# Layer norm of a recurrence writes its rows into the tile of the bounded rows, and the next load waits for the norm instead of the store

## The chip, the cores and the metric

One core of one Trainium2 chip runs the whole program: a TensorE (PE), a VectorE (DVE), a ScalarE (ACT), a GpSimd (POOL) and a SyncE (SP), which in this kernel only issues DMAs. The metric is the device time of one execution in microseconds (us).

## What is computed

Four layers on 2048 tokens of 512 channels, all in float32, each followed by a residual addition and a layer norm:

```python
x = layernorm(x + mamba2(x))              # first stage
x = layernorm(x + bounded_product(x))     # second stage, first half
x = layernorm(x + rg_lru(x))              # second stage, second half
x = layernorm(x + gated_ffn(x))           # third stage
```

The second stage, where the change lies, computes this:

```python
out = (x @ weight) * scale
n = max(norm(out), eps);  out = out * tanh(n) / (n + eps)
out = out * min(0.99 / max(norm(out), eps), 1)      # the bounded rows
x = layernorm(x + out)

y = gelu(x @ w_y + b_y);  xb = x @ w_x + b_x        # rg_lru
conv = causal convolution of xb over 4 tokens
gate_x, gate_a = sigmoid(conv @ w_ig + b_ig), sigmoid(conv @ w_ag + b_ag)
a = exp(-8 * gate_a * softplus(a_param));  mult = sqrt(1 - a**2)
h[t] = a[t] * h[t-1] + gate_x[t] * conv[t] * mult[t]
x = layernorm(x + (h * y) @ w_out + b_out)
```

## The kernel before, in words

The program has three stages, written as generators of instructions for each engine: `mamba2`, `bounded_rg_lru` and `gated_ffn`. The tokens go from stage to stage through HBM (tensors `tokens0`, `tokens1`). The order of the work on each engine is written out by hand, and engines are kept in step by counting semaphores. Every product is made of three passes over high and low parts of its operands (names that end in h and l).

The stage of the change is `bounded_rg_lru`. It works on NS = 8 pieces of 256 tokens, each of C = 2 chunks (j = 0, 1) of 128 tokens; pieces alternate between the two sequences. The loops of the engines' `main` run over steps s = 0 to 7, and a step mixes work for several pieces. The rows of a piece live in a row buffer, `slot(s)`, one of SLOTS = 3 tiles `c_xb` of 128 partitions x 2 chunks x 512. What happens to a piece p there:

- SP loads it from `tokens0` into its slot (`load_x`, L1091). Pieces 0 to 2 are loaded ahead; piece p = q + 3 takes the slot of piece q.
- In step p - 2 PE transposes its rows (`turn_in`, L1449), as the last work of the step; ACT copies the high part (L1201), DVE makes the low part (L1296).
- In step p - 1 PE multiplies it with the bounded layer's weights (L1456); DVE scales the result into the tile `ob` (`scaled`, L1301); ACT squares `ob` (L1206); POOL makes the bounding factors (L1135 to L1146); DVE adds the bounded row from `ob` to the row in the slot (`bounded`, L1308) and finishes that layer norm in place (`bounded_out`, L1317). From here `ob` is not used until the next step. PE transposes the slot again (`turn`, L1474), ACT and DVE make the parts `xth`, `xtl` (L1215, L1322), and POOL adds the output bias to the slot (L1161).
- In step p PE makes the four projections in the order x, y, ag, ig (`project`, L1486), with the bounded product of the next piece after x and the output product of the previous piece (`output`, L1456) after y. The ag projection waits for the convolution's high part `cvh` (ACT, L1263), the turn of the next piece stands between ag and ig.
- ACT makes the gates (L1224), the decay (L1233) and the square root (L1279). In step p + 1 DVE runs the recurrence (`recur`, L1350 to L1357), and late in the same step adds the product to the row in the slot (`norm`, L1368), and its last operation finishes the layer norm in place (`norm_out`, L1378).
- SP stores the finished rows from the slot to `tokens1` (`store`, L1096).

DVE's order in a step s is: recurrence of s - 1, `scaled` of s + 1, convolution of s (L1329), `bounded` and `bounded_out` of s + 1, `norm` and `norm_out` of s - 1, `turn` of s + 1, `turn_in` of s + 2, the square for the decay (L1344); at the end of steps 5 and 6 four conversions of the third stage's weight codes follow (`convert`, L1767).

ACT's order around the end of a step is: sigmoid of the ig projection (two halves, written to `gx`), the decay, the high part of `turn_in`, the square root.

SP has one queue of its own: `main` in its `sync` issues store(s) and then load_x(s + 3) for s = 0 to 4, store(5), then the next stage's transfers with store(6) and store(7) between them. The load of each chunk waits until the store of the same chunk has landed:

```python
wait(sp, s_st[j], 16 * (s - SLOTS + 1))
sp.dma_start(slot(s)[:, j, :], chunk(x_in, s, j)).then_inc(s_x[s % SLOTS][j], 16)
```

`wait` is a helper that emits nothing when the value is not positive. `order` makes the next instruction of an engine wait for the previous one. The third stage waits, before its first results are written, until all stores of the second have landed; its tile `d_sg` lies in the place of `ob`, and its residual tiles in the places of slots 0 and 1.

Of the kernel before, what the change touches and what calls it, by code (L numbers as in the profile page):

```python
# [12 lines left out]
ALU = mybir.AluOpType  # L13
# [36 lines left out]
class Again:  # L50
# [5 lines left out]
    def wait(self, eng, count):  # L56
        eng.wait_ge(self.sem, self.value + count)
# [939 lines left out]
def bounded_rg_lru(nc, signals, psum, ident, powers, x_in, x_out, scale, vectors, b_out, W, split, last, spaces, room, ahead):  # L997
# [7 lines left out]
    C = T // P  # L1005
    NT = x_in.shape[0] // (B * C)
    NS = B * NT
    M = KD
    SLOTS = 3
    TINY = 1e-7  # L1010
    LIMIT = 0.99
    def sem(name):
        return signals("c_" + name)
# [3 lines left out]
    for i in range(2):  # L1017
# [6 lines left out]
    ob = sb("c_ob", [P, C, D], F32)  # L1024
# [11 lines left out]
    mv = sb("c_mv", [P, C, 4], F32)  # L1036
# [29 lines left out]
    s_st = [sem(f"st{j}") for j in range(C)]  # L1066
# [7 lines left out]
    s_hy, s_hyh, s_hyl, s_bo, s_out, s_res, s_var, s_std, s_ln = (  # L1074
        sem(n) for n in ("hy", "hyh", "hyl", "bo", "out", "res", "var", "std", "ln"))
    s_dve, s_pool = sem("dve_order"), sem("pool_order")

    def chunk(dram, s, j):
        return dram[s % B * NT * C + s // B * C + j]
# [4 lines left out]
    def slot(s):  # L1084
        return xb[s % SLOTS]

    def sync(sp):
        def load_x(s):
            for j in range(C):
                wait(sp, s_st[j], 16 * (s - SLOTS + 1))  # L1090
                sp.dma_start(slot(s)[:, j, :], chunk(x_in, s, j)).then_inc(s_x[s % SLOTS][j], 16)  # L1091

        def store(s):
            for j in range(C):
                sp.wait_ge(s_ln, C * s + j + 1)
                sp.dma_start(chunk(x_out, s, j), slot(s)[:, j, :]).then_inc(s_st[j], 16)  # L1096

        def constants():
            sp.dma_start(vec, vectors).then_inc(s_small, 16)
            sp.dma_start(scl, scale.partition_broadcast(P)).then_inc(s_small, 16)  # L1100

        def main(following_stage):
            sp.wait_ge(*last["output"])
            sp.dma_start(bo, b_out.partition_broadcast(P)).then_inc(s_bias, 16)
            load_x(2)
            for dst, src, arrived in ahead:
                sp.dma_start(dst, src).then_inc(arrived, 16)
            for s in range(NS - 2):
                store(s)
                if s + SLOTS < NS:  # L1110
                    load_x(s + SLOTS)
            following_stage["small"]()
            following_stage["load_x"](0)
            following_stage["gate_codes"]()
            store(NS - 2)
            following_stage["up_codes"]()
            following_stage["load_r"](0, 0)
            following_stage["load_r"](0, 1)
            store(NS - 1)
            following_stage["down_codes"]()  # L1120
            for j in range(C):
                sp.wait_ge(s_st[j], 16 * NS)

        return {"load_x": load_x, "constants": constants, "main": main}

    def gpsimd(pool):
# [163 lines left out]
    def vector(dve):  # L1290
# [7 lines left out]
        def scaled(s):  # L1298
            for j in range(C):
                dve.wait_ge(s_bm, C * s + j + 1)  # L1300
                dve.tensor_tensor(ob[:, j, :], ps_o[:, j, :], scl, ALU.mult).then_inc(s_ob, 1)  # L1301

        def bounded(s):
# [70 lines left out]
        def norm_out(s):  # L1374
            for j in range(C):
                out = slot(s)[:, j, :]
                dve.wait_ge(s_std, C * s + j + 1)
                dve.tensor_scalar(out, out, mv[:, j, 0:1], mv[:, j, 2:3], ALU.subtract, ALU.mult).then_inc(s_ln, 1)  # L1378

        z = vec[:, AP, :]  # L1380
        e, u, l, one, q, k8 = (spt[:, i, :] for i in range(6))
# [19 lines left out]
        def main(following_stage):  # L1401
            dve.wait_ge(s_const, 1)
            for s in range(NS):
                if s:
                    recur(s - 1)
                    low_hy(s - 1)
                if s + 1 < NS:
                    scaled(s + 1)
                convolve(s)
                low_conv(s)  # L1410
                if s + 1 < NS:
                    bounded(s + 1)
                    bounded_out(s + 1)
                else:
                    following_stage["front"](0, (0, 1))
                if s:
                    norm(s - 1)
                    norm_out(s - 1)
                if s + 1 < NS:
                    turn(s + 1)  # L1420
                if s + 2 < NS:
                    turn_in(s + 2)
                if s + 1 == NS:
                    following_stage["front"](0, (2, 3))
                squared(s)
                if NS - 4 < s < NS - 1:
                    for i in range(4 * (s - NS + 3), 4 * (s - NS + 4)):
                        following_stage["convert"](i)
# [3 lines left out]
            for m in range(1, EARLY):  # L1432
                following_stage["product"](0, m)
            norm(NS - 1)
            norm_out(NS - 1)

        return {"turn_in": turn_in, "softplus": softplus, "scaled": scaled, "bounded": bounded, "bounded_out": bounded_out,
                "turn": turn, "main": main}

    def tensor(pe):  # L1440
# [58 lines left out]
        def main(following_stage):  # L1499
# [37 lines left out]
            "bias": (s_bo, C * NS), "gate_a": s_ga, "gate_x": s_gx, "n_gate": M * (NS - 1), "residual": s_res, "n_residual": C * (NS - 1),  # L1537
            "stored": s_st, "n_stored": 16, "steps": NS, "order": (s_dve, s_pool)}
    return (sync, gpsimd, scalar, vector, tensor), uses


# [336 lines left out]
def build(nc, x, out, d):  # L1878
# [7 lines left out]
    with ExitStack() as ctx:  # L1886
# [7 lines left out]
        for n, name in (("b", "weight"), ("x", "w_in1"), ("y", "w_y"), ("ag", "w_ag"), ("ig", "w_ig"), ("out", "w_out1")):  # L1894
# [9 lines left out]
        assert ends[0] == scan_at and place.at <= scan_at and late.at <= ends[1]  # L1904
        room["scan"] = scan_at
        second, last_second = bounded_rg_lru(nc, signals, psum, ident, powers, between[0], between[1], d["scale"], d["vectors"], d["b_out"], W,
                                dict(zip(W, parts)), last, ((place.at, scan_at), (ends[1], codes[0])), room,
                                [(dst, src, s_codes) for dst, src in transfers])
# [96 lines left out]
```

## Time and profile before

| what | value |
|---|---|
| three runs | 1181.51, 1182.25, 1185.72 us |
| median | 1182.25 us |
| the profiled execution, its own time | 1180.73 us |
| its span in the profile | 1178.9 us |
| PE busy | 1088.4 us (92%) |
| PE weight loads busy | 946.0 us (80%) |
| DVE busy | 748.2 us (63%) |
| ACT busy | 574.1 us (49%) |
| POOL busy | 320.2 us (27%) |
| share of the 16 DMA engines taken by SP's queue | 20.2% |

The span is the time from the first to the last recorded instruction; the execution's own time is 1.8 us longer. The first stage ends its PE work around 465 us, the stage of the change runs from there to about 805 us, the third stage to the end. Matmul durations overlap, since PE is pipelined; the starts of successive instructions tell more than their lengths.

### The profile page before, as it was taken

How to read it: one execution, taken by the hardware profiler on the slowest of the kernel's cores; microseconds unless marked ns; L12 is line 12 of the kernel's file. 1: busy time of each engine (PE TensorE's matmuls, PEld its weight loads, DVE VectorE, ACT ScalarE, POOL GpSimd, SP SyncE). 2: the span in 40 equal slices, each digit the busy share in tenths (PEclk: the TensorE clock that was granted, in tenths of full speed). 3: DMA queues.
4: the chain of work that ended last, by engine and by line, in shares of the span. 5: the costliest groups of instructions: out<-in, count | busy, mean ns of one | idle time of the engine just before them, and what ended most of it. 6: DMA issues, size and time to landing. Idle time of an engine off the chain costs nothing.

```text
span 1178.9 us, 18136 instructions
## 1 busy us (share of the span) xinstructions
PE 1088.4 (92%) x6912; PEld 946.0 (80%) x6912; DVE 748.2 (63%) x1307; ACT 574.1 (49%) x1190; POOL 320.2 (27%) x437
## 2 busy tenths in 40 slices
PE   6889999999999997599999999899999999999997
PEld 6778787978888885489898898887878878878876
DVE  6899999899999997548666776765332233223213
ACT  6866656666666654355666466563302311321320
POOL 1021213030312214453435344413302311321331
PEclk9899999999999998799999999989999999999999
DMA  5513131231303046220111101408012002002001
GB/s 189 194 41 101 46 96 51 91 104 38 122 20 122 7 147 229 94 95 1 37 37 37 36 1 36 136 18 285 1 36 72 1 18 90 1 1 72 1 1 54
DMA packets 41590, 81.22 MB, mean 69 GB/s; under 512 B 7456, under 2 KB 13472, under 8 KB 39456
## 3 DMA queue, kind: packets, MB, share of 16 engines
q1 hardware_dynamic: 41504, 80.06, 20.2%
q8 instruction: 55, 0.90, 0.3%
q14 instruction: 31, 0.25, 0.1%
HBM read 67.19 MB, written 12.85 MB: 68 GB/s over the span
## 4 chain that ended last, share of the span: by engine, by line
PE 64%; DVE 15%; ACT 10%; issue 5%; DMA 3%; POOL 3%; SPq 0%; DVEq 0%; POOLq 0%; ACTq 0%
PE banks L1836 20%; PE banks L799 17%; PE banks L1847 10%; PE banks L1486 7%; PE banks L1456 4%; DVE a_xs L698 2%; PE banks L879 1%; ACT a_xs L451 1%; DVE c_gx L1353 1%; PE banks L929 1%; DMA c_wxraw<-in_w_in 1%; DVE a_xs L691 1%; DVE a_L L675 1%; ACT c_a L1233 1%; DMA c_xb<-tokens 1%
## 5 line engine op out<-in xcount | busy, mean ns | idle before, releaser
L1737 ACT ACTIVATE d_sg<-banks,d_gs 128x512 f32<-128x512 f32 x64 | 44.0, 688 | 249.2 <-PE banks L1836 249.2
L1779 DVE SCALAR_TENSOR_TENSOR d_h<-banks,d_us,d_sg 128x512 f32<-128x512 f32 x64 | 48.0, 751 | 161.5 <-PE banks L1836 149.1
L1711 POOL TENSOR_TENSOR d_hl<-d_h,d_hh 128x512 fp32r<-128x512 f32 x64 | 83.1, 1298 | 156.0 <-ACT d_hh L1741 156.0
L1847 PE MATMUL banks<-d_wd,d_hh 128*128 128x512 f32 x256 | 104.1, 407 | 2.9 <-POOL d_hl L1711 2.9
L578 DVE SCALAR_TENSOR_TENSOR a_xs<-a_xpre,a_cvec,a_xs 128x256 f32<-128x256 f32 x192 | 100.3, 538 | 6.3 <-ACT a_xs L451 1.8
L1847 PE MATMUL banks<-d_wd,d_hl 128*128 128x512 f32 x256 | 103.6, 405 | 0.0
L327 POOL TENSOR_TENSOR a_sg<-a_sg 128x512 f32<-128x512 f32 x16 | 21.6, 1347 | 231.2 <-ACT a_sg L443 231.2
L661 DVE TENSOR_TENSOR_SCAN a_L<-a_L,a_ident 128x512 f32<-128x512 f32 x64 | 78.4, 1224 | 2.2
L467 ACT ACTIVATE a_xdt<-banks,a_dt 128x64 f32<-128x64 f32 x256 | 56.3, 349 | 47.2 <-PE banks L879 47.2
L799 PE MATMUL banks<-a_xth,a_wxh 128*128 128x256 f32 x256 | 75.9, 297 | 0.0
L799 PE MATMUL banks<-a_xth,a_wgh 128*128 128x256 f32 x256 | 74.7, 292 | 0.0
L799 PE MATMUL banks<-a_xtl,a_wxh 128*128 128x256 f32 x256 | 73.3, 286 | 0.0
L799 PE MATMUL banks<-a_xth,a_wxl 128*128 128x256 f32 x256 | 73.2, 286 | 0.0
L799 PE MATMUL banks<-a_xth,a_wgl 128*128 128x256 f32 x256 | 72.6, 283 | 0.0
L799 PE MATMUL banks<-a_xtl,a_wgh 128*128 128x256 f32 x256 | 72.5, 283 | 0.0
L1847 PEld LDWEIGHTS banks<-d_wd,d_hh 128*128 128x128 f32 x256 | 50.0, 196 | 14.8 <-POOL d_hl L1711 3.3
L799 PE MATMUL banks<-a_woh,a_ygh 128*128 128x512 f32 x128 | 57.5, 449 | 2.8 <-DVE a_ygl L704 2.8
L1847 PEld LDWEIGHTS banks<-d_wd,d_hl 128*128 128x128 f32 x256 | 49.8, 195 | 11.7
L1785 DVE TENSOR_TENSOR d_tmp<-banks,d_dsb 128x512 f32<-128x512 f32 x16 | 11.1, 691 | 75.5 <-PE banks L1847 75.5
L799 PE MATMUL banks<-a_woh,a_ygl 128*128 128x512 f32 x128 | 55.4, 432 | 0.0
L799 PE MATMUL banks<-a_wol,a_ygh 128*128 128x512 f32 x128 | 55.0, 430 | 0.0
L799 PEld LDWEIGHTS banks<-a_xth,a_wxh 128*128 128x128 f32 x256 | 49.7, 194 | 4.7 <-issue 4.0
(284 smaller groups left out, 3196.3 us busy)
## 6 DMA issues: line engine op xcount, KB each, us to landing
a_L<-decays SPq DMA_DIRECT2D x16, 1024.0 KB, 5.2
a_xf<-in_x SPq DMA_DIRECT2D x16, 256.0 KB, 2.9
a_xr<-in_x SPq DMA_DIRECT2D x16, 256.0 KB, 2.7
tokens<-a_xr SPq DMA_DIRECT2D x16, 256.0 KB, 4.2
c_xb<-tokens SPq DMA_DIRECT2D x16, 256.0 KB, 2.8
tokens<-c_xb SPq DMA_DIRECT2D x16, 256.0 KB, 2.0
d_xin<-tokens SPq DMA_DIRECT2D x16, 256.0 KB, 4.7
d_r<-tokens SPq DMA_DIRECT2D x16, 256.0 KB, 2.7
```

Source lines behind the costliest of these rows:

```text
L467: ins = act.activation(xdt[:, j, h * HD:(h + 1) * HD], ps_t[:, q % 2, 2 * j + i // 2, i % 2 * HD:(i % 2 + 1) * HD], ACT.Copy, scale=dt[:, ...
L578: ins = dve.scalar_tensor_tensor(out=dst, in0=src[:, k:k + T], scalar=vec[:, k:k + 1], in1=dst, op0=ALU.mult, op1=ALU.add)
L661: order(dve.tensor_tensor_scan(own, own, ident4.rearrange("p h t -> p (h t)"), 0.0, ALU.mult, ALU.add))
L698: dve.tensor_tensor(own, own, sg[:, :, cols(j)], ALU.mult).then_inc(s_yg, 1)
L799: last = pe.matmul(out, lhs(i, k), rhs(c, k), start=(k, i, c) == (0, 0, 0), stop=(k, i) == (n - 1, 1))
L1456: done = pe.matmul(ps_x, x[:, k, cols(j)], wp[:, k, :], start=i == 0, stop=i == 3 * KD - 1)
L1486: done = pe.matmul(ps_x[:, q, m % 2, :], wp[:, k, m * P:(m + 1) * P], x[:, k, :], start=i == 0, stop=i == 3 * KD - 1)
L1711: pool.tensor_tensor(hl[:, m, :], h32[:, m % 2, :], hh[:, m, :].bitcast(F32), ALU.subtract).then_inc(s_hl, 1)
L1737: act.activation(sg[:, m % 2, :], ps_g[:, m % 2, :], ACT.Silu, scale=gs[:, m:m + 1]).then_inc(s_sg, 1)
L1779: dve.scalar_tensor_tensor(out=h32[:, m % 2, :], in0=ps_u[:, m % 2, :], scalar=us[:, m:m + 1], in1=sg[:, m % 2, :], op0=ALU.mult, op1=ALU. ...
L1836: ins = pe.matmul(out[:, m % 2, :], w(k, m), x[:, k, :], start=(k == 0 and x is xth), stop=(k == KD - 1 and x is xtl))
L1847: ins = pe.matmul(ps_o[:, c % 2, :], h[:, m, cols(c)], wd[:, m, :], start=(m == 0 and h is hh), stop=(m == M - 1 and h is hl))
```

## The change

The last operation of the layer norm (`norm_out`) writes pieces 0 to 4 into `ob` instead of the slot, and SP stores those from `ob`. Pieces 5 to 7 are written and stored as before. The load into the slot waits for `norm_out` of the old piece and no longer for its store, and SP issues it ahead of that store. `scaled`, which is the next to write `ob`, gets a wait for that store.

```diff
     def slot(s):
         return xb[s % SLOTS]
 
+    def finished(s):
+        return ob if s + SLOTS < NS else slot(s)
+
     def sync(sp):
         def load_x(s):
             for j in range(C):
-                wait(sp, s_st[j], 16 * (s - SLOTS + 1))
+                wait(sp, s_ln, C * (s - SLOTS) + j + 1)
                 sp.dma_start(slot(s)[:, j, :], chunk(x_in, s, j)).then_inc(s_x[s % SLOTS][j], 16)
 
         def store(s):
             for j in range(C):
                 sp.wait_ge(s_ln, C * s + j + 1)
-                sp.dma_start(chunk(x_out, s, j), slot(s)[:, j, :]).then_inc(s_st[j], 16)
+                sp.dma_start(chunk(x_out, s, j), finished(s)[:, j, :]).then_inc(s_st[j], 16)
...
             for s in range(NS - 2):
-                store(s)
                 if s + SLOTS < NS:
                     load_x(s + SLOTS)
+                store(s)
...
         def scaled(s):
             for j in range(C):
                 dve.wait_ge(s_bm, C * s + j + 1)
+                wait(dve, s_st[j], 16 * (s - SLOTS + 1))
                 dve.tensor_tensor(ob[:, j, :], ps_o[:, j, :], scl, ALU.mult).then_inc(s_ob, 1)
...
-                dve.tensor_scalar(out, out, mv[:, j, 0:1], mv[:, j, 2:3], ALU.subtract, ALU.mult).then_inc(s_ln, 1)
+                dve.tensor_scalar(finished(s)[:, j, :], out, mv[:, j, 0:1], mv[:, j, 2:3], ALU.subtract, ALU.mult).then_inc(s_ln, 1)
```

## Rows read from the trace of the kernel before

**Rows 1.** The page: the span, and the chain that ended last by engine.

```profile
span 1178.9 us, 18136 instructions
PE 64%; DVE 15%; ACT 10%; issue 5%; DMA 3%; POOL 3%; SPq 0%; DVEq 0%; POOLq 0%; ACTq 0%
```

**Rows 2.** The chain of waits in order of time (start us, us, what), 530 to 800 us.

```profile
561.29 2.02 DMA tokens<-c_xb
563.33 2.71 DMA c_xb<-tokens
566.08 0.66 PE banks L1449 x4
...
635.52 2.00 DMA tokens<-c_xb
637.54 2.88 DMA c_xb<-tokens
640.46 0.66 PE banks L1449 x4
...
710.07 2.00 DMA tokens<-c_xb
712.09 2.64 DMA c_xb<-tokens
714.77 0.65 PE banks L1449 x4
```

**Rows 3.** Waits of PE, the whole span (us in total, times, longest us).

```profile
PE banks L1449 <- DMA c_xb<-tokens: 7.1, 9, 1.6
```

**Rows 4.** Timeline of PE, second chunk of turn_in at the end of steps 2 and 4.

```profile
602.56 0.65 PE L1449 MATMUL banks<-ident,c_xb 128*128 128x128 f32 x4 [0.75 <-DMA c_xb<-tokens]
...
677.50 0.66 PE L1449 MATMUL banks<-ident,c_xb 128*128 128x128 f32 x4 [0.79 <-DMA c_xb<-tokens]
```

**Rows 5.** Timeline of ACT, the last ig gate of steps 0 to 6.

```profile
527.07 0.84 ACT L1224 ACTIVATE c_gx<-banks,c_vec 128x256 f32<-128x256 f32 x2 [2.00 <-PE banks L1486]
...
563.12 0.84 ACT L1224 ACTIVATE c_gx<-banks,c_vec 128x256 f32<-128x256 f32 x2 [2.00 <-PE banks L1486]
...
601.33 0.84 ACT L1224 ACTIVATE c_gx<-banks,c_vec 128x256 f32<-128x256 f32 x2 [2.00 <-PE banks L1486]
...
638.02 0.84 ACT L1224 ACTIVATE c_gx<-banks,c_vec 128x256 f32<-128x256 f32 x2 [2.00 <-PE banks L1486]
...
675.90 0.84 ACT L1224 ACTIVATE c_gx<-banks,c_vec 128x256 f32<-128x256 f32 x2 [2.00 <-PE banks L1486]
...
712.96 0.84 ACT L1224 ACTIVATE c_gx<-banks,c_vec 128x256 f32<-128x256 f32 x2 [2.00 <-PE banks L1486]
...
750.23 0.84 ACT L1224 ACTIVATE c_gx<-banks,c_vec 128x256 f32<-128x256 f32 x2 [2.00 <-PE banks L1486]
```

**Rows 6.** Timeline of DVE: norm_out of the second chunk, steps 1 and 3.

```profile
560.72 0.55 DVE L1378 TENSOR_SCALAR c_xb<-c_xb,c_mv 128x512 f32<-128x512 f32 x1 [0.71 <-POOL c_mv L81]
...
634.95 0.55 DVE L1378 TENSOR_SCALAR c_xb<-c_xb,c_mv 128x512 f32<-128x512 f32 x1 [0.71 <-POOL c_mv L81]
```

**Rows 7.** Timeline of the weight loads: PE's wait for cvh in step 1.

```profile
550.21 0.53 PEld L1486 LDWEIGHTS banks<-c_cvh,c_wagh 128*128 128x128 f32 x4 [0.29 <-ACT c_cvh L1263]
```

**Rows 8.** Timeline, steps 5 and 6: conversion, bounded_out (DVE), turn (PE).

```profile
719.75 0.68 DVE L1767 TENSOR_SCALAR d_wg_early<-d_wg_early_codes 128x1024 fp32r<-128x1024 int32 x1
...
742.97 0.55 DVE L1317 TENSOR_SCALAR c_xb<-c_xb,c_bmv 128x512 f32<-128x512 f32 x1 [0.72 <-POOL c_bmv L81]
...
743.48 1.03 PE L1474 MATMUL banks<-ident,c_xb 128*128 128x128 f32 x8
```

**Rows 9.** Timeline: scaled in step 5, PE's wait for hyl in step 7.

```profile
691.58 1.28 DVE L1301 TENSOR_TENSOR c_ob<-banks,c_scl 128x512 f32<-128x512 f32 x2
...
767.11 0.80 PE L1456 MATMUL banks<-c_wouth,c_hyh 128*128 128x512 f32 x1 [4.68 <-DVE c_hyl L1361]
```

**Rows 10.** DMA issues of two lines with their times to landing.

```profile
L1091 SPq DMA_DIRECT2D c_xb<-tokens x16: 319/320/1757, 436.7 to 712.1; - x16
...
DMA to landing us min/median/max: 2.6/2.8/10.7
...
L1659 SPq DMA_DIRECT2D d_xin<-tokens x16: 430/432/2561, 750.5 to 990.1; - x16
...
DMA to landing us min/median/max: 2.7/4.7/11.9
```

**Rows 11.** Stretches, steps 1 and 2: length, busy PE PEld DVE ACT POOL, PEclk, DMA, GB/s.

```profile
527.00:563.00 36.00, 35.96 (x257) 33.35 (x255) 25.64 (x48) 21.84 (x40) 14.69 (x24) 1.00 0.04 16
563.00:601.00 38.00, 35.66 (x256) 33.29 (x256) 25.61 (x48) 22.06 (x40) 15.45 (x24) 1.00 0.11 37
```

## The prediction
> **What bounds the kernel now.** The page's chain that ended last comes first: PE holds 64% of it, and DMA 3% [rows 1]. The chain in order of time then says where those DMAs are. In the stage of the change it has three passes of one form, at 561, 636 and 710 us: a store of 2.0 us, at once the load that waited for it (2.6 to 2.9 us), and then PE's `turn_in` [rows 2]. The list of PE's waits gives the price: `turn_in` waited 7.1 us for these loads in total [rows 3]. That is a ceiling seen from PE; seen from the chain the ceiling is its three stores, 2.02 + 2.00 + 2.00 = 6.0 us, since a chain can't become shorter than what is cut from it. No other wait inside the steps 1 to 6 is of that size; after them PE waits 4.7 us for the recurrence [rows 9], which hangs on the gates of step 6. So what decides is how much earlier step 6 ends.
>
> I measure the stage by G(n), the start of the last ig gate on ACT in step n, which follows the last ig matmul at once: G(0) to G(6) are 527.07, 563.12, 601.33, 638.02, 675.90, 712.96, 750.23 [rows 5]. Four quantities make them:
>
> - Step 0 to 1 had its load early, and its length of 36.05 is a **floor** for every step. Its first ag weight load still waited 0.29 us for `cvh` [rows 7], so PE alone would be near 35.7.
> - The loop over ACT, DVE and POOL: `norm_out` of the second chunk ends 561.27 and 635.50 [rows 6], that is G(n-1) + 34.2 both times (561.27 - 527.07, 635.50 - 601.33).
> - From that end to T, the start of `turn_in`'s second chunk: 566.08 - 561.27 = 4.81, 640.46 - 635.50 = 4.96 [rows 2, 6].
> - From T to the next G: 35.25, 35.46, 35.44, 35.46, 35.46 (601.33 - 566.08 to 750.23 - 714.77) [rows 2, 4, 5].
>
> So a step's G depends on the G two steps earlier: 34.2 + 4.9 + 35.4 = 74.5 us for two steps, where the floor is 72.1. PE and the DVE loop nearly balance, and the store sits on the link between them.
>
> **The change part by part.** *The load no longer waits for the store*: five pairs of loads (pieces 3 to 7). The interval from `norm_out` to T loses its store, so it is 2.8 to 3.0 us. I go through the steps, T' and G' being the new times:
>
> - Step 1: T' = 561.27 + 2.79 = 564.06, G'(2) = 564.06 + 35.25 = 599.3.
> - Step 2: T' = 563.12 + 34.2 + 2.96 = 600.3, G'(3) = 635.7.
> - Step 3: T' = 599.3 + 34.2 + 2.96 = 636.5, G'(4) = 671.9.
> - Step 4: T' = 635.7 + 34.2 + 3.03 = 672.9, G'(5) = 708.4.
> - Step 5: T' = 671.9 + 34.2 + 2.72 = 708.8, and by the same rule G'(6) = 744.3.
>
> The floor holds in all of them within 0.2 us (599.3 - 563.1 = 36.2 and so on). **What is late next** is in step 6. Four conversions of about 0.6 us stand before its recurrence on DVE [rows 8], so `bounded_out`'s second chunk ended at 743.52, G(5) + 30.56, just as PE's `turn` began with the first chunk at 743.48. G'(5) comes 4.5 us earlier, but PE reaches `turn` 5.9 us earlier and must wait for that row. From the second half of `turn` (0.4 after 743.48) to 750.23 are 6.3 us, so G'(6) = 708.4 + 30.56 + 6.3 = 745.3. That is 750.23 - 745.3 = 4.9 us of gain, and 5.9 without this wait.
>
> After G(6) everything in the stage follows from the gates, PE even has its 4.7 us of slack before `hyl` [rows 9], and the third stage runs on PE back to back, so the shift goes through whole. PE's granted clock is already 1.00 in these steps [rows 11], so nothing is won or lost there: what PE did before is the same.
>
> *The store moves behind the load in SP's order.* SP issues two loads, then two stores, 0.32 us each. The load of the second chunk was alone in flight, or nearly; now two stores leave 0.3 and 0.6 us behind it. Nearest rows: the load of the first chunk today goes out while the second chunk's store is in flight, and all loads of this line have a median of 2.8; four loads issued in a row (`d_xin`) land after 2.7 at least and 4.7 in the median [rows 10]. So between 0 and +1.9 us for each load, and I take 0.05, because what is behind it in the queue should hardly hurt the transfer ahead, and the 2.7 is the nearest row. Three of them are on the chain: 0.15. The stores themselves land up to 1 us later, read by nobody in time.
>
> The Trainium skill, "DMA: Bandwidth & Descriptors", section on latency and other measured facts, puts an HBM access at 0.2 us on average and 2 us at high load. If the two stores made such a load, the landing would grow by up to 1.8 us and an estimate by it would leave almost no gain; the first-chunk loads of today's trace, which meet a store and don't show it, speak against that.
>
> *`scaled` gets a wait*: for pieces 3 to 7, two chunks, ten waits on DVE. Behind it on DVE stand the convolution and all that follows. The store leaves at G(n-1) + 34.2 + about 0.7 and lands 2 us later, near G(n) + 1; `scaled` runs at G(n) + 15.7 (691.58 - 675.90) [rows 9]. The wait is met with some 14 us to spare. A satisfied wait has no row of its own; it costs between 0 and the 0.1 us of the smallest gaps in the chain, I take 0.03, for six of them on the path 0.2 us.
>
> *`norm_out` writes another tile*: same shape and type, 0.55 us [rows 6], nothing. `ob` is free there: its readers, ACT's square and DVE's `bounded`, come earlier in the same step.
>
> **Sum.** 4.9 - 0.15 - 0.2 = 4.55 us. The profiled execution took 1180.73, so 1176.2; the median of the runs stands 1.5 us above it, which gives 1182.25 - 4.6 = 1177.6.
>
> **The rivals.**
>
> - *A, the whole chain*: PE's new wait in step 6 doesn't appear, or the loads land a little faster, and the gain is the three stores, 6.0: 1176.2. For it: 7.1 us of PE's waits are there to be removed. Against it: `bounded_out` in step 6 is fixed by DVE.
> - *B, the loads pay back part*: the stores right behind them cost each load on the chain 0.8 us, 2.4 in all, leaving 2.3: 1180.0. The median of 4.7 for four in a row speaks for it, the pair's 2.8 against.
> - *C, slower*: the same place, worse. From 4.7 / 3 = 1.6 us more per load on, the gain is gone; if a load with two stores beside it takes double, 5.6 instead of 2.8, the sum is 3 x 2.8 - 4.7 = 3.7 us slower: 1186.0. The largest landing of this line, 10.7 us, was with megabytes of weights in flight [rows 10], where now there are two stores.
> - *D, no effect*: the load was not what held PE, for instance because PE waits as long for `cvh` and `turn` instead: 1182.3. The waits of 0.29 us in the only step without a late load [rows 7] speak against more than a tenth of it.
>
> **How the numbers follow.** 0.5% is 5.9 us, about what a measurement of this kernel can tell from no change. The forecast has 0.55 (own range, 4.0 to 5.4 of gain: 1176.8 to 1178.3), A 0.20, B 0.13, C 0.05, D 0.07. The gain's ceiling of 6.0 lies at that bound, so "faster" is half of A and, with the 1.5 us between execution and median, a part of the forecast: 0.25. "Slower" is most of C: 0.04. The rest, 0.71, is "same", though I expect a real gain there. The range reaches from a little under A, 1175.2, to past B, 1180.8; out of it stay C and D and a tail of A, 0.2 in all.
>
> **What the profile would show.** Right: SP's load is issued within 0.1 us of `norm_out`'s end; the chain has no DMA `tokens<-c_xb` in this stage; PE's wait at L1449 falls from 7.1 to about 2 us; G spacings near 36.2; PE waits 0.5 to 1.5 us at L1474 in step 6; G(6) near 745.5; landings of L1091 stay 2.6 to 2.9. Wrong: landings over 3.5 us (B, C); new waits of PE at L1474 or L1486 in every step (D); DVE waiting for a DMA at L1301; or G(6) moved by 4.6 and the end not, which would mean that the third stage waits for something of its own.

## The result, and the profile after

| | before | changed |
|---|---|---|
| runs | 1181.51, 1182.25, 1185.72, 1185.07 us | 1175.85, 1175.38, 1176.04, 1174.91 us |
| median | 1183.66 us | 1175.62 us |
| the profiled execution, its own time | 1180.73 us | 1175.85 us |
| its span | 1178.9 us | 1174.1 us |
| PE busy | 1088.4 us | 1085.9 us |

The ratio is 0.9932, with a 95% interval from 0.991 to 0.9954. The changed kernel is faster by 8.0 us between the medians, but by 4.8 us of span between the two profiled executions. These are two findings. The traces can explain the second number directly; what lies between it and the first is taken up below.

The chain of waits of the changed kernel in order of time (start us, us, what), 590 to 810 us, answers to [rows 2]:

```profile
597.05 3.30 DMA c_xb<-tokens
600.35 0.04 issue
600.39 0.65 PE banks L1453 x4
...
670.04 2.97 DMA c_xb<-tokens
673.01 0.04 issue
673.05 0.66 PE banks L1453 x4
...
724.47 0.90 issue
725.36 1.28 DVE c_ob L1305 x2
726.64 1.59 DVE c_cv L1333 x4
...
731.67 1.07 ACT c_cvh L1266
732.76 1.24 DVE c_cvl L1341
734.00 0.04 issue
734.04 5.06 PE banks L1490 x40
```

No store is in it any more, and two loads are left where there were three pairs of store and load. But a load now takes 3.30 and 2.97 us where it took 2.64 to 2.88. The last lines show the new last wait, in step 6: PE stands at the ag projection until DVE's convolution and its low part are there. (Line numbers are 3 to 4 higher than before: L1453 is `turn_in`, L1490 `project`, L1382 `norm_out`.)

PE's waits of the changed kernel, 526 to 750 us (us in total, times, longest us), say the same:

```profile
PE banks L1453 <- DMA c_xb<-tokens: 3.4, 5, 1.1
PEld banks L1490 <- ACT c_cvh L1266: 0.7, 2, 0.5
PEld banks L1490 <- DVE c_cvl L1341: 0.7, 3, 0.3
```

Against [rows 3], 7.1 us fell to 3.4, and the small waits of the weight loads (PEld) for `cvh` and `cvl`, 0.3 and 0.2 us before, grew to 0.7 each.

The timeline of ACT, the last ig gate of steps 0 to 6, answers to [rows 5]:

```profile
526.74 0.84 ACT L1227 ACTIVATE c_gx<-banks,c_vec 128x256 f32<-128x256 f32 x2 [2.00 <-PE banks L1490]
...
562.82 0.84 ACT L1227 ACTIVATE c_gx<-banks,c_vec 128x256 f32<-128x256 f32 x2 [2.00 <-PE banks L1490]
...
599.79 0.84 ACT L1227 ACTIVATE c_gx<-banks,c_vec 128x256 f32<-128x256 f32 x2 [2.00 <-PE banks L1490]
...
635.85 0.84 ACT L1227 ACTIVATE c_gx<-banks,c_vec 128x256 f32<-128x256 f32 x2 [2.00 <-PE banks L1490]
...
672.34 0.84 ACT L1227 ACTIVATE c_gx<-banks,c_vec 128x256 f32<-128x256 f32 x2 [2.00 <-PE banks L1490]
...
708.50 0.84 ACT L1227 ACTIVATE c_gx<-banks,c_vec 128x256 f32<-128x256 f32 x2 [2.00 <-PE banks L1490]
...
745.68 0.84 ACT L1227 ACTIVATE c_gx<-banks,c_vec 128x256 f32<-128x256 f32 x2 [2.00 <-PE banks L1490]
```

From G(0) to G(6) are 218.94 us; before they were 223.16. So 4.2 of the 4.8 us arise here. Another 0.3 us lie ahead of G(0) (527.07 and 526.74) and 0.3 us after G(6) (428.67 and 428.42), where the change does nothing. Other executions differ there by more: a second trace of the changed kernel has 426.71 us after G(6) and a span of 1172.7 (experiment 1), a second one of the kernel before 427.05 and 1179.4 (experiment 11). So the 4.2 us of the stage are the firm number, and the 4.8 us are one pair of executions; the four spans taken crosswise differ by 4.8 to 6.7 us. In the sections below, "the stage" is this distance from G(0) to G(6).

DVE's timeline of the changed kernel at the end of step 2, and then SP's, show the new order:

```profile
596.48 0.55 DVE L1382 TENSOR_SCALAR c_ob<-c_xb,c_mv 128x512 f32<-128x512 f32 x1 [0.71 <-POOL c_mv L81]
```

```profile
595.79 1.58 SPq L1094 DMA_DIRECT2D c_xb<-tokens  x2
597.42 0.90 SPq L1099 DMA_DIRECT2D tokens<-c_ob  x2
```

The first load goes out right after the first chunk's layer norm, the second at 597.05, 0.02 us after the second one's end (596.48 + 0.55), and the two stores 0.4 us behind it.

### The profile page after: what moved, and what is told of

Same layout as the page of the kernel before. It is cut to its first block, busy times and chain, and to the rows that moved or that the text cites. A ratio compares the mean times of both kernels' runs of the same rounds, so it can differ in the third digit from the quotient of the medians.

```text
span 1174.1 us, 18146 instructions
## 1 busy us (share of the span) xinstructions
PE 1085.9 (92%) x6912; PEld 943.6 (80%) x6912; DVE 747.9 (64%) x1307; ACT 574.3 (49%) x1190; POOL 323.4 (28%) x437
## 4 chain that ended last, share of the span: by engine, by line
PE 62%; DVE 17%; ACT 10%; issue 5%; DMA 2%; POOL 2%; SPq 0%; DVEq 0%; POOLq 0%; ACTq 0%
PE banks L1840 20%; PE banks L799 17%; PE banks L1851 11%; PE banks L1490 7%; PE banks L1460 2%; DVE a_xs L698 2%; DVE c_cv L1333 2%; PE banks L879 1%; ACT a_xs L451 1%; DVE c_gx L1357 1%; PE banks L929 1%; ACT c_a L1236 1%; DMA c_wxraw<-in_w_in 1%; DVE a_xs L691 1%; DVE a_L L675 1%
```

## The experiments

The experiments ran in four sets (1 to 4, 5 to 8, 9 to 11, and 12), each on a chip of its own together with runs of the kernel before, which had medians of 1182.33, 1182.43, 1183.08 and 1183.17. Each median is compared with the one of its own set. "The stage" is read from each one's trace.

**1. The changed kernel again.** No edit.

> The changed kernel once more, paired with the kernel before in five rounds. The two traces differ by 4.8 us of span (1178.9 and 1174.1), of which 4.2 us arise between the gates of step 0 and step 6; the medians differ by 8.0. Theory 1, the link alone: the difference of the medians comes out near 4.8 (ratio 0.996). Rival: the kernel before has something besides that the two profiled executions don't show, such as loads that land late in some executions, and the difference stays near 8 (ratio 0.993), with its runs scattered over 3 to 4 us and those of the changed kernel within 1.5 us.

The median was 1175.51 (six runs, 1174.29 to 1176.06), that of the kernel before 1182.33 (22 runs, 1180.46 to 1189.3), the ratio 0.9933 (0.9911 to 0.9954). So the difference of 7 us is real, and of these two kernels the one before is the one that scatters: its shortest runs are 5 us above the changed kernel's median, its longest 14. The stage took 219.04 us, as in the first trace of the changed kernel.

**2. Only the tile and the new wait.**

```diff
-                wait(sp, s_ln, C * (s - SLOTS) + j + 1)
+                wait(sp, s_st[j], 16 * (s - SLOTS + 1))
...
             for s in range(NS - 2):
+                store(s)
                 if s + SLOTS < NS:
                     load_x(s + SLOTS)
-                store(s)
```

> Only the tile of norm_out and the new wait of scaled are kept; the load again waits for the store and stands behind it. Theory 1: nothing is gained, the time is that of the kernel before within 1.5 us, the load goes out 2.0 us after the store of its chunk, and PE waits about 7 us at turn_in. DVE waits for no store at scaled. Rival, the changed destination or the free slot is itself worth or costs something: more than 2 us from the kernel before.

Ratio 0.9999 (0.9982 to 1.0016), stage 223.28 us, PE's wait at `turn_in` 7.5 us. Writing to `ob` and ten more waits on DVE cost nothing that can be measured and bring nothing. So the gain comes from when the load goes out.

**3. The stores first.**

```diff
             for s in range(NS - 2):
+                store(s)
                 if s + SLOTS < NS:
                     load_x(s + SLOTS)
-                store(s)
```

> The whole change but for SP's order: both stores are issued, then both loads, which wait for the layer norm alone. The load of the second chunk, the one on the chain, goes out 1.0 to 1.3 us after norm_out instead of at once (two issues of 0.32 to 0.43 us more), with both stores ahead of it in the queue. Theory 1: its way from norm_out to turn_in takes 4.0 to 4.5 us, 0.8 to 1.2 more than in the changed kernel, and three such ways make it 2.5 to 3.5 us slower than the changed kernel. Rival, the order is nothing and only the wait counted: within 1 us of the changed kernel.

Median 1177.95 (nine runs, 1175.8 to 1182.17), 2.4 us over the changed kernel of the same set; stage 221.15 against 219.04 us. SP's timeline of this kernel at the end of step 1, and then PE's:

```profile
560.20 1.58 SPq L1099 DMA_DIRECT2D tokens<-c_ob  x2
561.82 0.94 SPq L1094 DMA_DIRECT2D c_xb<-tokens  x2
```

```profile
564.88 1.39 PE L1453 MATMUL banks<-ident,c_xb 128*128 128x128 f32 x8 [1.65 <-DMA c_xb<-tokens]
```

The second load goes out near 562.3, 0.9 us after `norm_out`'s end (560.88 + 0.55 = 561.43), and the loads on the chain land after 3.27, 3.08 and 2.98 us. A start 0.8 us later on a way that the chain takes three times makes 2.4 us. The order on SP is worth a third of the change by the medians (2.4 of 6.8 us) and half of it by the stage (2.1 of 4.2).

**4. No loads at all.** Pieces 3 to 7 are not loaded; they are computed from what the slot holds.

```diff
             for s in range(NS - 2):
-                if s + SLOTS < NS:
-                    load_x(s + SLOTS)
                 store(s)
...
         def turn_in(s):
             for j in range(C):
-                pe.wait_ge(s_x[s % SLOTS][j], 16 * (s // SLOTS + 1))
+                if s < SLOTS:
+                    pe.wait_ge(s_x[s][j], 16)
+                else:
+                    pe.wait_ge(s_ln, C * (s - SLOTS) + j + 1)
```

(In `bounded`, DVE's own wait for these loads is left out too.)

> The loads of pieces 3 to 7 are left out, and PE's turn_in and DVE wait for the layer norm of the old piece instead; those pieces are computed from what the slot holds. It gives the end of this road: the link without any DMA. Theory 1: every step takes the floor of 36.05 us, or 35.9 to 36.3, so steps 1 to 6 take 3 us less at most than in the changed kernel (whose gates of steps 1 to 6 are 182.9 us apart), 180.3 to 181.5, and the time is 1.3 to 2.6 us under the changed kernel's. PE waits for cvh and cvl by 0.3 to 0.8 us in each step and not for turn_in. Rival, DMA is still the bound of the stage: 4 us or more are gained.

Median 1173.04 (four runs, 1171.93 to 1176.43), stage 217.57 us, gates of steps 1 to 6 181.49 us apart. PE's waits in it:

```profile
PEld banks L1492 <- ACT c_cvh L1264: 2.5, 6, 0.5
PEld banks L1492 <- DVE c_cvl L1340: 1.5, 6, 0.3
```

All spacings but the last are 36.03 to 36.09 us, the last, with the conversions in front of it, is 37.26. So the floor of 36.05 is real; the only wait that PE has in each of its steps is the one for the convolution's two parts, and the changed kernel is 1.4 us of stage from this one. With nothing left to load, the store's removal could not have brought more than 223.16 - 217.57 = 5.6 us of stage.

**5. Stores held until the loads have landed.**

```diff
                 if s + SLOTS < NS:
                     load_x(s + SLOTS)
+                    sp.wait_ge(s_x[s % SLOTS][1], 16 * ((s + SLOTS) // SLOTS + 1))
                 store(s)
```

> The changed kernel, but SP issues the two stores only when both loads have landed, so that the loads are alone in flight. It measures what the stores right behind the loads cost. In the changed kernel the way from norm_out's end to turn_in's second chunk was 3.36, 3.36 and 3.04 us where steps 1, 2 and 4 waited, against 2.7 to 2.9 from issue to landing of a load that was alone. Theory 1: the way falls back to 2.8 to 3.0 us, the gates of steps 1 to 6 come 0.5 to 1.2 us closer (floor of 36.05 in every step), and the time falls by as much. Rival, the load is slower for another reason (it reads at once what was just written, or its issue): the way stays at 3.3.

The loads of the chain land after 2.77 and 2.76 us again, from 3.30 and 2.97; PE's wait at `turn_in` is 2.1 us from 3.4; the stage 218.22 from 218.94. The median was 1173.63 (four runs, 1172.04 to 1176.92), ratio 0.9928 (0.9905 to 0.9951), which overlaps the changed kernel's interval: a gain of the whole time is not shown. The loads bear the step out in other traces: the seven on the chain with stores right behind them (the changed kernel twice, experiment 6) took 2.97 to 3.33 us, the four with held stores (this one and experiment 8) 2.69 to 2.77. So the stores right behind the load cost it 0.2 to 0.6 us. The ten stores from `ob` took 3.6 us in the median in the changed kernel and 2.3 here.

**6. The conversions moved, in the changed kernel.**

```diff
                 if s + 1 < NS:
                     turn(s + 1)
+                if NS - 4 < s < NS - 1:
+                    for i in range(4 * (s - NS + 3), 4 * (s - NS + 4)):
+                        following_stage["convert"](i)
                 if s + 2 < NS:
                     turn_in(s + 2)
                 if s + 1 == NS:
                     following_stage["front"](0, (2, 3))
                 squared(s)
-                if NS - 4 < s < NS - 1:
-                    for i in range(4 * (s - NS + 3), 4 * (s - NS + 4)):
-                        following_stage["convert"](i)
```

> The changed kernel with the eight conversions of the third stage's codes moved on DVE ahead of the low part of turn_in, where DVE sits idle 5 us in each step for ACT, instead of after the square for the decay. Theory 1: with the store out of the link the DVE loop is what spaces the steps, and four conversions of 0.6 us stood in it in step 5 and four, 3.6 us, in step 6. Step 5 to 6 (37.2 us between gates in the changed kernel) falls to about 36.1, the recurrence of step 6 comes about 2 us earlier after the last gate, and the time falls by 2.5 to 3.5 us. Rival, PE is the bound there anyway and the conversions are hidden: within 1 us of the changed kernel.

The trace shows the places as foreseen: step 5 to 6 took 36.65 us instead of 37.18, and the recurrence of step 6 began 7.4 us after G(6) instead of 9.1. From G(0) to PE's output product in step 7 the trace has 233.46 us instead of 235.81. Yet the median, 1174.63 (1172.27 to 1176.17), is only 0.9 us under the changed kernel's; with a ratio of 0.9929 (0.9913 to 0.9945) the two can't be told apart. The expectation of 2.5 to 3.5 us was missed in the runs; up to that product the trace shows 2.4.

**7. The same move in the kernel before.**

> The same move of the conversions in the kernel before the change. Theory 1: in step 6 the same 2 us, in step 5 less or nothing of the rest, because there the load is what the step waited for only until its turn_in and the conversions come after it: 1.5 to 3.5 us under the kernel before. If it gains the same as in the changed kernel, the two are additive; if nothing, the store's link covered the conversions.

Median 1178.91 against 1182.43, ratio 0.997 (0.9959 to 0.9982): 3.5 us faster. Why the same move brings 3.5 us here, and nothing clear of noise in experiment 6, is not shown. Its trace brought the surprise of this study. The stage took 226.93 us, with spacings of 40.45 and 39.64 us for steps 1 to 2 and 3 to 4, where the code is that of the kernel before, which had 38.21 and 37.88. PE's timeline of `turn_in` at the end of step 1 and after it:

```profile
563.64 0.66 PE L1449 MATMUL banks<-ident,c_xb 128*128 128x128 f32 x4 [1.84 <-DMA c_xb<-tokens]
565.29 0.66 PE L1449 MATMUL banks<-ident,c_xb 128*128 128x128 f32 x4 [0.99 <-DMA c_xb<-tokens]
565.70 0.88 PE L1486 MATMUL banks<-c_xth,c_wxh 128*128 128x256 f32 x4
566.37 1.06 PE L1486 MATMUL banks<-c_xth,c_wxl 128*128 128x256 f32 x4
567.23 1.05 PE L1486 MATMUL banks<-c_xtl,c_wxh 128*128 128x256 f32 x4
568.08 1.05 PE L1486 MATMUL banks<-c_xth,c_wxh 128*128 128x256 f32 x4
568.94 0.89 PE L1486 MATMUL banks<-c_xth,c_wxl 128*128 128x256 f32 x4
569.67 0.64 PE L1486 MATMUL banks<-c_xtl,c_wxh 128*128 128x256 f32 x4
```

Groups of four matmuls start 0.86 us apart from 566.4 to 569 and 0.47 us apart from 569.7 on. The granted clock of 566.1 to 569.5 us is 0.50: TensorE ran at its lower level, 1.2 GHz, for some 3 us after it had stood idle twice for the loads (1.84 and 0.99 us), and then at 2.4 GHz again; from `turn_in` to the next gate are 37.0 us (602.29 - 565.29) instead of 35.25, so this fall cost 1.7 us.

**8. Both, the moved conversions and the held stores.**

> Both, the moved conversions and the held stores, on top of the change. Theory 1: the gains add up where the floor leaves room, 3 to 4.5 us under the changed kernel, and the gates of steps 1 to 6 are 180.3 to 181 us apart. Rival: one of the two replaces the other, 2.5 us or less.

Median 1171.47 (five runs, 1170.97 to 1172.87), ratio to the kernel before 0.9908 (0.9892 to 0.9923), 2.2 under experiment 5 of the same set and 4.0 us under the changed kernel's 1175.51, which is of another set (none of its runs is as short as this version's longest). The stage took 217.34 us, and its gates of steps 1 to 6 are 181.29 apart. This version is the fastest of the study and computes the same.

**9. PE kept busy in the wait, in the kernel before.**

```diff
-                pe.wait_ge(s_x[s % SLOTS][j], 16 * (s // SLOTS + 1))
...
+                if s >= SLOTS:
+                    for k in range(6 - 2 * j):
+                        pe.transpose(ps_t[:, j, k % KD, :], ident, ident)
+                pe.wait_ge(s_x[s % SLOTS][j], 16 * (s // SLOTS + 1))
```

(the wait for the load is moved behind the wait for the bank and the spare transposes.)

> The kernel before, but PE runs ten spare transposes of the identity (six ahead of the first chunk, four ahead of the second) where it stands idle for the loads of pieces 3 to 7. Clock theory: in some executions of the kernel before, TensorE's granted clock falls to half for 3 us after the wait at turn_in (seen in the trace of the run with the conversions moved in the kernel before: 0.96 over steps 1 to 2 and 3 to 4, matmuls of 128x256 at 0.21 us instead of 0.12 from 566 to 570 us), which makes such a step 1.7 us longer; that is why its runs spread over 5 to 9 us, and why the medians lie 7 apart and the traces 4.8. With the idle time filled, the clock stays at 1.00, the runs spread over 3 us or less, and the median comes down 1.5 to 2.5 us, to 1180 to 1181, without the load coming earlier. Rival, the spread comes from DMA: the same median and spread as the kernel before.

The median was 1183.3, the ratio 1.0001 (0.9984 to 1.0018), the runs 1179.15 to 1186.45. The trace has a granted clock of 1.00 in every step and, once, a store of the chain that took 3.75 us instead of 2.0. So what the clock theory expected did not come: PE's waits at `turn_in` fell to 4.0 us, from 7.1 to 7.7, and the median did not come down. Its stage took 225.22 us in this trace, 2.1 more than in the first trace of the kernel before, 1.75 of them by that one store; whether the spare transposes lengthen other executions is not known, so the theory is weakened and not refuted.

**10. One longer wait, in the kernel before.**

```diff
                 wait(sp, s_st[j], 16 * (s - SLOTS + 1))
+                wait(sp, s_st[C - 1], 16 * (s - SLOTS + 1))
```

> The kernel before, but the load of the first chunk waits for both stores, so it goes out 1.3 us later and PE's wait at turn_in is in one piece, 0.5 to 3 us, instead of two. Clock theory: the granted clock falls in two or three of the steps in each execution, and the median rises by 3 us or more, of which the later load itself explains 1 at most (0.3 us a step on the second chunk). Rival without a clock: 1 us slower or less.

Median 1185.02, ratio 1.0017 (1.0002 to 1.0032), 1.9 us slower. In the trace PE's timeline at the end of step 1 reads:

```profile
565.51 0.66 PE L1450 MATMUL banks<-ident,c_xb 128*128 128x128 f32 x4 [3.08 <-DMA c_xb<-tokens]
566.59 0.65 PE L1450 MATMUL banks<-ident,c_xb 128*128 128x128 f32 x4 [0.42 <-DMA c_xb<-tokens]
567.00 1.10 PE L1487 MATMUL banks<-c_xth,c_wxh 128*128 128x256 f32 x4
567.89 1.05 PE L1487 MATMUL banks<-c_xth,c_wxl 128*128 128x256 f32 x4
568.75 1.05 PE L1487 MATMUL banks<-c_xtl,c_wxh 128*128 128x256 f32 x4
569.60 1.05 PE L1487 MATMUL banks<-c_xth,c_wxh 128*128 128x256 f32 x4
570.46 0.68 PE L1487 MATMUL banks<-c_xth,c_wxl 128*128 128x256 f32 x4
```

After 3.08 and 0.42 us of idle time the clock fell to 1.2 GHz, and the step took 41.09 us. It fell in one step of this execution, not in two or three, and the 1.9 us lie between what the clock theory expected (3 or more) and the rival (1 or less).

**11. The kernel before once more.**

> The kernel before once more with a profile, for a second look at it. Clock theory: if its time is over 1183, its trace shows a step of 38.5 us or more between gates with a granted clock under 1.00; if it is near 1180.5, none does. The loads land after 2.8 us in the median either way. Rival: a slow execution has late loads or a longer first or third stage.

Its profiled execution took 1181.18 us. Steps 1 to 5 are like those of [rows 5], but step 5 to 6 took 39.61 us instead of 37.27. PE's timeline there:

```profile
713.94 0.66 PE L1449 MATMUL banks<-ident,c_xb 128*128 128x128 f32 x4 [1.24 <-DMA c_xb<-tokens]
715.33 1.08 PE L1449 MATMUL banks<-ident,c_xb 128*128 128x128 f32 x4 [0.73 <-DMA c_xb<-tokens]
716.05 1.20 PE L1486 MATMUL banks<-c_xth,c_wxh 128*128 128x256 f32 x4
717.06 1.05 PE L1486 MATMUL banks<-c_xth,c_wxl 128*128 128x256 f32 x4
```

The fall is in the unedited kernel too, and this expectation failed in its other half: an execution near 1180.5 was to have none. The loads landed as ever (2.8 us).

**12. The old wait without the store, in the changed kernel.** The loads go out late by a signal of POOL and no longer hang on the store's landing.

```diff
-                wait(sp, s_ln, C * (s - SLOTS) + j + 1)
+                wait(sp, s_delay, C * (s - SLOTS) + j + 1)
...
+                if 0 < s <= NS - SLOTS:
+                    for j in range(C):
+                        pool.wait_ge(s_ln, C * (s - 1) + j + 1)
+                        part = bo[:, 0:(384, 240)[j]]
+                        order(pool.tensor_tensor(part, part, powers[:, 3:4].broadcast_to(part.shape), ALU.mult))
+                        pool.tensor_tensor(part, part, powers[:, 3:4].broadcast_to(part.shape), ALU.mult).then_inc(s_delay, 1)
+                        pool.wait_ge(s_delay, C * (s - 1) + j + 1)
```

(SP's order is again store, then load.)

> Stores from ob as in the changed kernel, but each load goes out about 2 us after its chunk's layer norm, on a signal of POOL (two multiplications of a part of the output bias by -1, for each chunk) and not on the store's landing. So PE waits at turn_in as long as in the kernel before, while no store's landing stands on the chain. It tells apart two causes for the 2 to 3 us by which the medians of the kernel before stand above its profiled executions, and for its spread (29 runs from 1179.95 to 1190.02, with a mean granted clock of 0.97 to 0.959, the slow ones lower). Clock after the longer waits: the median is 1181.5 to 1184, its runs spread over 5 us or more and correlate with the granted clock. Stores that sometimes land late (3.75 us instead of 2.0 in one trace): the median is 1179.5 to 1181.5 and the runs spread over 3 us or less, as the changed kernel's do.

Median 1183.79 against 1183.17 of the kernel before, runs from 1181.54 to 1185.66, correlation of time and mean granted clock -0.68 (-0.78 in the 17 runs of the kernel before in this set). The loads of the chain went out 2.0 us after the end of `norm_out`, as meant; but its operation on the second chunk, which runs beside POOL's multiplications here, took 1.04 us instead of 0.55 in each of the five steps. On three passes this makes 1.5 of the 2.1 us by which the stage, 225.25, was longer. The profiled execution took 1181.98 and had no fall; the median stands 1.8 us above it, as in the kernel before. So the excess of the medians is there without any store on the chain, and late stores are not needed for it.

## Why the prediction was right, and where it was not

**The link and its arithmetic: right, with 0.7 us less in the stage.** The two-step loop of layer norm, store, load and `turn_in` was what spaced the steps. Measured from G(0), the forecast had G(2) to G(6) at 72.2, 108.6, 144.8, 181.3 and 218.2 us, the trace has 73.05, 109.11, 145.60, 181.76 and 218.94. The rival "no effect" is refuted by that, and rival A, the whole 6.0 us, in the stage by experiment 4: even without loads only 5.6 are to be had. The working has 4.9 us of gain in the stage before its two small costs, and 4.2 were measured. PE's wait at `turn_in` was to fall to about 2 us and fell to 3.4.

**The new destination and the waits of `scaled`: right**, by experiment 2; 0.2 us were set aside for them, and nothing was measured.

**The store behind the load: right in kind, too small.** The step set 0.05 us for each load, "because what is behind it in the queue should hardly hurt the transfer ahead". It measured 0.2 to 0.6 us (3.30 and 2.97 against 2.77 and 2.76 in experiment 5), and the forecast that landings stay at 2.6 to 2.9 us failed with it. Rival B's 0.8 us was too much. The Trainium skill, "DMA: Bandwidth & Descriptors", section on latency and other measured facts, gives 2 us for an HBM access under high load. No run here shows such a load: beside the two stores of 256 KB a load's landing grew by 0.6 us at most.

**The wait in step 6: right in size, wrong in place.** The forecast had PE wait at `turn` (L1474) for `bounded_out`. PE waited earlier, at the ag projection, for `cvh` (0.24 us before the first weight load) and `cvl` (0.25), and came to `turn` late enough not to wait. The same delayed DVE chain holds both: the forecast asked only the later of its two customers. Step 5 to 6 took 37.18 us where the working gives 36.9.

**The third stage: the shift goes through** (428.67 and 428.42 us from G(6) to the end), but that the two agree so well is luck, and PE is not quite "back to back" there: at four places it stands idle for 2.0 to 2.9 us. Stretches of 20 us around them in the trace of the kernel before (length, busy PE PEld DVE ACT POOL, PEclk, DMA, GB/s):

```profile
850.00:870.00 20.00, 18.01 (x79) 14.50 (x78) 7.03 (x12) 4.00 (x7) 3.83 (x5) 0.91 0.01 1
940.00:960.00 20.00, 18.01 (x79) 14.40 (x78) 4.83 (x7) 6.18 (x11) 5.13 (x4) 0.91 0.00 1
1036.00:1056.00 20.00, 17.64 (x78) 14.09 (x77) 4.83 (x7) 5.31 (x10) 5.13 (x4) 0.91 0.01 2
1130.00:1150.00 20.00, 17.10 (x74) 13.48 (x73) 2.25 (x3) 4.25 (x7) 5.11 (x4) 1.00 0.00 0
```

A clock of 0.91 over 20 us is one fall to 1.2 GHz of some 3 us. All fourteen traces, of either kernel, have two or three such falls at these four places. In the eleven traces that leave the conversions alone, 426.7 to 427.2 us lie between G(6) and the end with two falls and 428.3 to 428.8 with three: a fall costs about 1.6 us here. The two profiled executions of the result happen to have three each.

**The time itself: too high by 2 us.** The measured 1175.62 lies within the stated range, 1175.2 to 1180.8, but below the forecast's own, 1176.8 to 1178.3, and it is nearest to the 1176.2 of rival A, whose reason did not come true; that it still lies in the range is in part luck. 4.6 us of gain were forecast, 4.8 are in the spans; but the medians differ by 7 to 8. The step that failed is the one between the profiled execution and the median: "the median of the runs stands 1.5 us above it, which gives 1182.25 - 4.6". That excess was taken as a constant of both kernels. The changed kernel has little of it: its ten runs reach from 1174.3 to 1176.1, close to its own profiled executions (1175.85 and 1174.55), where the 22 and 29 runs of the kernel before reach from 1180 to 1190. With it fails "nothing is won or lost there", which was said of the clock from the rows of two steps in one execution.

What makes the excess is narrowed down, not settled. Shown is: it goes with the granted clock (correlation -0.74 over 29 runs; their eight shortest have a mean granted clock of 0.966, the eight longest 0.962). One fall costs 1.6 to 1.7 us, 0.0014 of the mean clock, so this difference would be two or three falls more in the long ones, about 4.4 of the 6.1 us between the two groups; that is an estimate from these numbers. TensorE fell to 1.2 GHz after `turn_in` in experiments 7 (twice), 10 and 11, each such step 1.8 to 2.9 us longer than in [rows 5], and in none of the seven traces of kernels whose loads don't wait that long (the changed kernel twice, experiments 3, 4, 5, 6, 8). The excess doesn't need the store on the chain (experiment 12). Against a simple story stand the falls in the first and third stages, which the changed kernel has as well; the runs of experiments 3, 4 and 5, which scatter by 6.4, 4.5 and 4.9 us with less waiting at `turn_in` (4.6 us, none and 2.1 us in their traces); experiment 9, where filling almost half of the idle time didn't help; and the first trace of the kernel before and those of experiments 2 and 12, with waits as long or longer and no fall. Where the long executions lose their clock is open: no trace of one over 1182 us was taken of the kernel before.

## What to carry to other kernels

Where a load waits for the store of the same buffer, look whether that pair is on the chain, and give the finished rows another tile that happens to be empty: the load can then go out with the last read, 2 us earlier, and it should be issued ahead of the stores (a third to a half of the gain here). Holding the stores back until it has landed made the loads 0.2 to 0.6 us faster; what that alone brings to the whole time is not shown. Work out the gain as a recurrence over the steps, with a floor from a step that didn't have the wait, and ask each customer of the delayed engine, the earliest first. When a change takes idle time from PE, compare the scatter of the runs too: part of the gain may lie in the executions that the trace doesn't show. And before two spans are subtracted, count the falls of the clock in both traces: here one more or less outside the changed stage moved a span by about 1.6 us.

## What the runs showed of the hardware

- After two idle times of 1.50 and 0.59 us (experiment 7), or 1.24 and 0.73 us (experiment 11), with four short transposes between, TensorE's clock fell to 1.2 GHz for about 3 us, and after 1.59 and 0.75 us (the kernel before), or even 2.10 and 0.87 us (experiment 12), it did not. In the third stage it fell after a wait of 1.99 us near 952 us in the kernel before and not after one of 1.99 us at the same place in experiment 2, where in turn it fell after 2.90 us near 1140 us and in the kernel before did not. So the length of the gap alone does not decide; what does, no run here shows.
- Such a fall made the work of PE that it hit 1.6 to 1.7 us longer.
- A store of 256 KB from this stage lands after 2.0 us in the kernel before, and after 3.6 us in the median (3.9 at most) where two of them are issued right behind a load; the load ahead of them loses 0.2 to 0.6 us.
- POOL's multiplication of 128x384 by a broadcast column took 0.83 to 0.89 us and that of 128x240 0.59 us, and DVE's last operation of the layer norm, which ran beside them, 1.04 us instead of 0.55 (experiment 12).
